# A decoder layer in which the selective scan puts four states of 32 channels on the partitions, and GpSimd's product waits for one thing fewer

## The reference

```python
# 1. linear attention, 16 heads of 32, in chunks of 128 tokens
q, k, v = x @ Wq, x @ Wk, x @ Wv               # then rotary on q and k
out = (q*decay) @ kv + ((q @ k.T) * dmask) @ v # kv carried from chunk to chunk
x1  = norm(x + rms_norm(out) @ Wo)
# 2. a selective scan over ctx [4, 512, 256]: 512 channels, 16 states each
u   = silu(causal_conv(ctx @ in_w.T) + conv_b)
dt_low, Bm, Cm = split(u @ xp_w.T)             # 16 + 16 + 16 rows per token
dt  = softplus(dt_low @ dt_w + dt_b)
for t in range(512):
    state = state * exp(dt[t]*A) + (dt[t]*u[t])[:, None] * Bm[t]  # [512, 16]
    y[t]  = sum over the 16 states of state * Cm[t]
x2  = norm(x1 + (y + D*u) * silu(x1))
# 3. 64 experts of width 192, top 8, capacity 256 rows each
w, e = top_8(softmax(x2 @ router.T));  slots from the counts so far
out  = norm(x2 + sum of w * expert_e(x2))
```

## Time and profile before

| | us |
|---|---|
| runs shown (3) | 1634.18 median, 1626.55 to 1635.15 |
| profiled execution | 1628.64 |
| its span, first to last instruction | 1626.8 |
| DVE busy | 1154.4 (71%) |
| PE busy | 1257.4 (77%) |
| POOL busy | 971.2 (60%) |
| ACT busy | 846.7 (52%) |
| mean granted TensorE clock | 0.886 |

### The profile page before, as it was taken

The page is one execution under the profiler, slowest core; times in us unless marked ns, Lnnn a source line. Parts: engine busy times, 40 slices in busy tenths (PEclk is TensorE's granted clock), DMA queues, the critical chain, the costliest instruction groups (busy, mean ns, idle before and its releaser), DMA issues. The chain is left out here.

```text
span 1626.8 us, 19387 instructions
## 1 busy us (share of the span) xinstructions
PE 1257.4 (77%) x6567; PEld 850.5 (52%) x6567; DVE 1154.4 (71%) x1554; ACT 846.7 (52%) x1417; POOL 971.2 (60%) x740
## 2 busy tenths in 40 slices
PE   1697998877898787888777661099999999999960
PEld 1243544444444353344443341099988888888850
DVE  0277988769787768877786743088878878878855
ACT  1455555642365534366423320078777777777742
POOL 0148646563886645885738824447776766767741
PEclk9978998978998898998888865589999999999985
DMA  9155545363585353664543420389999999999978
GB/s 336 66 195 183 209 146 215 134 220 110 131 205 197 110 207 123 154 197 170 192 142 108 162 82 1 102 243 304 303 294 296 292 294 292 291 294 294 292 142 309
DMA packets 146705, 326.92 MB, mean 201 GB/s; under 512 B 19504, under 2 KB 55232, under 8 KB 146480
## 3 DMA queue, kind: packets, MB, share of 16 engines
q1 hardware_dynamic: 113280, 258.41, 49.6%
q0 software_dynamic: 32768, 67.26, 17.3%
q10 hardware_dynamic: 560, 0.02, 0.0%
HBM read 273.20 MB, written 52.43 MB: 200 GB/s over the span
## 5 line engine op out<-in xcount | busy, mean ns | idle before, releaser
L849 POOL TENSOR_TENSOR dbu<-bmat,dtu 128x1024 f32<-128x1024 f32 x128 | 301.9, 2363 | 178.8 <-PE y_ps L315 62.6
L990 DVE TENSOR_TENSOR_SCAN hst<-hst,dbu 128x512 f32<-128x512 f32 x256 | 299.3, 1215 | 140.5 <-POOL dbu L849 109.0
L315 PE MATMUL y_ps<-dbu,cs 128*128 128x512 f32 x512 | 288.5, 693 | 102.3 <-DVE y L1006 63.8
L1484 POOL DMA_INDIRECT sum_rows<-ye,tokens x128 | 205.5, 1606 | 117.3 <-ACT ye L1554 88.1
L315 PEld LDWEIGHTS y_ps<-dbu,cs 128*128 128x128 f32 x512 | 101.9, 213 | 223.4 <-issue 103.0
L628 ACT ACTIVATE hst<-dt,a_sc 128x512 f32<-128x512 f32 x256 | 165.8, 683 | 90.6 <-DVE dbu L998 90.1
L364 PE MATMUL ring<-wqkv,xT 128*128 128x512 f32 x384 | 189.2, 639 | 23.7 <-DVE x L1065 13.2
L1476 POOL DMA_INDIRECT xe<-x_rows,tokens x128 | 159.4, 1246 | 56.3 <-issue 37.7
L926 POOL DMA_INDIRECT slot_table<-pairs,idx_s x128 | 125.6, 981 | 111.4 <-DVE idx_s L1159 73.4
L1618 DVE TENSOR_TENSOR w1l<-w,w1h 128x1024 fp32r<-128x1024 f32 (+1 forms) x128 | 117.2, 957 | 76.7 <-ACT w1h L1567 53.6
L998 DVE TENSOR_TENSOR dbu<-hst,cmat 128x1024 f32<-128x1024 f32 x128 | 156.7, 1224 | 11.0 <-DMA cmat<-bc_rows 6.7
(11 more groups left out here) (207 smaller groups left out, 2627.4 us busy)
## 6 DMA issues: line engine op xcount, KB each, us to landing
bmat<-bc_rows SPq DMA_DIRECT2D x128, 512.0 KB
cmat<-bc_rows SPq DMA_DIRECT2D x128, 512.0 KB
w<-in_L_ffn_gate_up_proj SPq DMA_DIRECT2D x64, 768.0 KB
w<-in_L_ffn_down_proj SPq DMA_DIRECT2D x64, 256.0 KB
w<-in_L_ffn_down_proj SPq DMA_DIRECT2D x128, 128.0 KB
rows<-sum_rows SPq DMA_DIRECT2D x8, 1024.0 KB, 12.9
sum_rows<-junk SPq DMA_DIRECT2D x1, 4608.0 KB, 23.8
x_in<-in_x SPq DMA_DIRECT2D x16, 256.0 KB, 4.1
```

Source lines behind the costliest of these rows:

```text
L315: ins = pe.matmul(y_ps[:, :], ident, dbu[:, n % WORK, i, :], start=(k == 0 and i == 0), stop=(k == UNIT - 1 and i == 1))
L849: pool.tensor_tensor(dbu[:, n % WORK, :, :], bmat[:, n % BSETS, :, :], dtu[:, m, :].unsqueeze(1).broadcast_to([P, 2, T]), ALU.mult).then_i ...
L990: dve.tensor_tensor_scan(h, h, dbu[:, n % WORK, i, :], 0.0, ALU.mult, ALU.add).then_inc(scanned, 1)
L1484: pool.indirect_dma_start(sum_dram[e % SUMS], bass.IndirectOffsetOnAxis(ap=tokens[:, e, j:j + 1], axis=0), ye[:, e % YE, j, :], None, comp ...
```

## The change

**Layout of the scan.** A slot now holds one quad of states (k = 0 to 3) of two groups of 32 channels: partition = 4 states x 32 channels, and the free dimension is 2 groups x 512 tokens. A unit is two halves (64 channels each) of four slots, so it has 8 slots as before, with two scans of 128x512 in each. `bmat` and `cmat` have a place for each quad and are loaded once per sequence: 4 transfers of 32 partitions for each of B and C and quad. In exchange `dt` and `dt*u` must stand four times below one another: SP copies them from SBUF to SBUF, 8 transfers of 64 KB each for `dt_rep` and 8 for `dtu_rep` per half (`spread_steps`, `spread_inputs`), double buffered, issued up to a half ahead. PE sums the four states by a product with `sel` (128x32, ones where p mod 32 matches), one per 32 channels, into 32 rows of `y_ps`. All four waits of `inputs` but the one for `scanned` have a counterpart.

**Set-up.** The block `setup` is gone. The host hands over weights already laid out (`layout`), x and ctx also transposed, so that PE does not turn them; the zeros go out in unit 1 (`clear_sums`); ACT scales `wo` (`weigh_rows`) after the first decays.

**Order.** `EARLY` is m = 0, 1 and `LATE` m = 2, 3. The next sequence's context projection and convolution sit in slots 0 to 5 of c = 2, `project_u` at its end; `second_sum` and `soft_rest` move one place back. `scatter` sends one store per slot from slot 2 of c = 2 on, through c = 3 and the next sequence's c = 0 and c = 1 (two or three per slot in the last sequence's c = 2 and c = 3).

```diff
-UNIT = PAIRS
+UNIT = 2 * QUADS
-EACH = 3
-EARLY, LATE = (0,), (1, 2, 3)
+EARLY, LATE = (0, 1), (2, 3)
@@ PE, sum_states
-                for i in range(2):
-                    pe.wait_ge(yc_ready, products(2 * n + i + HSTATES))
-                    ins = pe.matmul(y_ps[:, :], ident, dbu[:, n % WORK, i, :], start=(k == 0 and i == 0),
-                                    stop=(k == UNIT - 1 and i == 1))
+                pe.wait_ge(yc_ready, products(2 * n + 2))
+                for g in range(2):
+                    rows = slice((2 * half + g) * QP, (2 * half + g + 1) * QP)
+                    ins = pe.matmul(y_ps[rows, :], sel, dbu[:, n % WORK, g, :], start=(k == 0), stop=(k == QUADS - 1))
@@ SP
-                sp.dma_start(bmat[:, n % BSETS, :, :], bc_dram[b, 2 * k:2 * k + 2, :].partition_broadcast(P))\
+                for s in range(4):
+                    sp.dma_start(bmat[s * QP:(s + 1) * QP, k, :], bc_dram[b, 4 * k + s, :].partition_broadcast(QP))\
+            def spread_steps(b, m, half):
+                i = spread_of(b, m, half)
+                sp.wait_ge(dt_ready, softened(b, m))
+                wait(sp, da_ready, 2 * QUADS * (i - 1))
+                for g in range(2):
+                    for s in range(4):
+                        sp.dma_start(dt_rep[s * QP:(s + 1) * QP, i % 2, g, :],
+                                     dt[(2 * half + g) * QP:(2 * half + g + 1) * QP, m, :]).then_inc(dt_spread[i % 2], 16)
@@ POOL, inputs
                 if k == 0:
-                    pool.wait_ge(dtu_ready, softened(b, m))
+                    spread(pool, dtu_spread, i)
-                pool.wait_ge(b_loaded[n % BSETS], 16 * (n // BSETS + 1))
+                pool.wait_ge(b_loaded[k], 64 * (b + 1))
                 wait(pool, summed, n - WORK + 1)
-                wait(pool, scanned, 2 * (n - 2) + 1)
-                pool.tensor_tensor(dbu[:, n % WORK, :, :], bmat[:, n % BSETS, :, :],
-                                   dtu[:, m, :].unsqueeze(1).broadcast_to([P, 2, T]), ALU.mult).then_inc(dbu_ready, 1)
+                pool.tensor_tensor(dbu[:, n % WORK, :, :], dtu_rep[:, i % 2, :, :],
+                                   bmat[:, k, :].unsqueeze(1).broadcast_to([P, 2, T]), ALU.mult).then_inc(dbu_ready, 1)
@@ POOL, scatter
-                        if b and c >= 2:
-                            at = UNIT * (c - 2) + k
-                            scatter(b - 1, EACH * at, EACH * (at + 1))
+                        if b and c >= 2 and UNIT * c + k >= 2 * UNIT + 2:
+                            each = 1 if not last else 2 if c == 2 or k >= 4 else 3
+                            scatter(b - 1, sent, sent + each)
+                            sent += each
+                        if b >= 2 and c < 2:
+                            each = 2 if c == 1 and k >= 6 else 1
+                            scatter(b - 2, sent, sent + each)
+                            sent += each
@@ ACT, take_mixed and take_rows
-                if t == 0:
-                    act.wait_ge(zeros_stored, 16 * (1 + SUMS))
+                if b == 0 and j == 0:
+                    act.wait_ge(zeros_stored, 16 * (1 + SUMS))
+                    act.wait_ge(table_cleared, 16)
```

632 lines of the change are left out of this document (332 added, 300 removed).

## The result

The changed kernel takes 1586.53 us (median of 4 runs, 1583.99 to 1592.61), the kernel before beside it 1630.62. The ratio is 0.973, 95% interval 0.969 to 0.978: 44 us faster. The forecast was 1523, a gain of 108 against that median. The time is inside the range, at its upper end (1588); less than half of the gain came.

What follows compares the result with a forecast made beforehand. DVE was taken to bound the loop, with its waits on top. Span 1626.8 less 26 (start) and 85 (loop 868 to 783) gives 1516, plus 7 for the median: 1523 us, range 1465 to 1588.

Steps and rivals of the forecast that it cites:

- the table: Predicted unit times in the loop: c = 0 at 44.5 to 46, c = 1 58 to 60, c = 2 52, c = 3 44.5.
- Start, -26: Before the loop: ctx loaded earlier, so POOL's first product comes at 54.4 instead of 80.4 us, gain 26.
- The copies of a half ... cost nothing there: In the loop: dt and dt*u copies are issued four slots ahead, so that lead hides them at no cost.
- the handover at 8.3 against 9 us: Where c = 3 passes to the next batch: copies take 8.3 us, hidden by two DVE slots of about 9.
- POOL or the handover: Rival, chance 0.15: POOL's load and the handover keep c = 0 and c = 3 as they were; 1559 us.
- (g): POOL's dropped wait for `scanned`: PE's sum still holds the product, so counted at 0, between -14 and +15 us.
- POOL's free product blocks DVE: Rival, chance 0.04: POOL's product, out of step with the scans, meets the q and k turns; 14 us more, 1537.
- PE's sum, -115: PE's sum over states: two column parts run at once, so PE loses about 115 us, bounds 0 and 115.
- no overlap: Rival, chance 0.06: PE's column parts do not overlap at N = 512; a third of 115 on the path, 1561 us.
- (a) to (e): Reordering in units: turned-y wait 9.2 to 1.5, slot 8's wait 7.54 to 1, c = 2's 8 us of waits gone.
- (f): Routing step in c = 1: PE's and DVE's waits (5.88 and 7.35 us) stay; only C's late rows go.
- 665 to 685: Sign to check the forecast: DVE's busy time in the loop, in us, within a loop of 760 to 810.

Runs made afterwards that it cites:

- x1: The changed kernel with the loads of lane and wo issued before the first rows are stored: 1568.86 us.
- x3: The changed kernel with the dropped wait put back (POOL's product waits for the scan two slots back): 1568.33 us.
- x12: x5 with B's and C's rows loaded for batch 0 only, not again at the handovers (later batches lack their own rows): 1523.35 us.
- x5: The changed kernel with lane and wo loaded earlier, the dropped wait back, and all quad 2 and 3 rows ahead of the copies: 1552.68 us.
- x7: The kernel before without POOL's wait for the scan two slots back, nothing else: 1633.60 us, ratio 1.0034.
- x8: The changed kernel with POOL's table stores as before, three per slot in c = 2 and c = 3: 1603.72 us.
- x11: x5 with each matmul of PE's sum issued twice, so y comes out doubled: 1571.94 us.
- x4: The kernel before with PE's sum taking only the even state of each pair: 1605.52 us, ratio 0.984.
- x6: x5 with ACT making slot 5's exponentials before copying q out, in c = 1 of batches 1 to 3: 1552.51 us.
- x9: x5 with each quad of B's or C's rows loaded by one 256 KB transfer instead of four of 64 KB: 1551.84 us.
- x10: x9 with x's tiles issued ahead of the copies and C's quads 2 and 3 issued by ACT: 1554.52 us.

## Why the prediction was wrong, point by point

The forecast missed by 63.5 us. The runs name three losses: the last loads 17.7 (x1), the dropped wait 18.2 (x3), the rows at the handovers 29.3 (x12 against x5), 65 when added up. x12, which has none of the three, is 63.2 below the changed kernel, at 1523.35.

That this is the forecast's very number is luck in part. The forecast was a span of 1516 and 7 for the median above it, and here the median is 2.3 above the profiled span (0.7 in x12). The span was missed by 68: the first scan came 19.6 late (76.3 for 56.7), the loop took 43.7 more (826.7 for 783), and 5 came behind it. Of the loop's part the c = 0 units have 34.5 (171.0 for 136.5) and the c = 1 units 20.8 (198.8 for 178); the rest came out 7 under the table, and the 5 added for the clock were not needed. In x12, too, the first scan is 4.5 late (61.2), the c = 1 units take 12.7 more than the table (190.7) and the stages behind the loop 5.5 more, and what was put too high elsewhere makes up for it.

1. *Start, -26.* Right in its steps: rows of xdbl at 30.4 for 29.4, first product at 58.7 for 54.4; the 4.3 us between are mostly the copies, 0.63 us to issue for the 0.41 taken from the loads of rows. Wrong where it ended: I followed the chain to POOL's product and took the scan for its next link, without reading what stands ahead of the scan on DVE. `lane` was in the same queue as `wo`, one entry later, and I priced only `wo` (8).

2. *"The copies of a half ... cost nothing there", and the handover at 8.3 against 9 us.* This is the step that failed by most: it priced the copies alone, and the rows' reload at nothing. I compared the copies with DVE's lead and forgot that the rows of quads 2 and 3 stand in the same queue, behind them. The runs show 29.3 us for the reload (x12), and that turning the order round does not win it back: with all rows ahead of the copies (x5) c = 0 stays at 54.3 to 54.5. The rival "POOL or the handover", which had 0.15, has the right place and a wrong cause: it named POOL's load, and it kept c = 0 and c = 3 as they were. The loss is in c = 0, behind the batch's end; c = 3 is 1.4 us over the table.

3. *(g) The dropped wait, counted at 0, bounds -14 to +15.* It is +18, outside both. The rival "POOL's free product blocks DVE" (0.04, +14) named the mechanism, an instruction of DVE held while one of POOL runs, and nearly the size, but its instructions were the turns of q and k, which x3 shows unchanged (its L1035 is 488 ns now with and without the wait, while the two instructions ahead of it went from 1124 to 1515). The stretched ones are those of the routing step. I gave it 0.04 although showed L1035 at three times its twin; what kept the product beside the scans was the very wait that the change removes. That the two were one thing I did not see. The argument for 0, that `summed` holds the product anyway, is what x7 shows of the kernel before, with 5 us for 18; the change made the sum half as long in the same step.

4. *c = 1 at 60.* Measured 65 to 67. x3 alone gives 61.1 to 63.7, x8 alone 60.6: the rest is most likely the stores, moved beside the routing step (about 2.5).

5. *PE's sum, -115.* Close as busy time (-118.6), with luck: half of 2.25 us a slot is 144 over 128 slots, and the 0.9 in the sum comes from no row. PE's lower clock most likely took the difference back. The forecast gave it no line of its own; "no overlap" priced a third of it, 38. Its worth is 19 to 25 us (x11, x4). Before, c = 2 of the later batches did not depend on it at all (x4); with the stores gone it does by 2 to 3.5 us (52.5 twice in x11, 49.0 and 50.5 in x5). With less work PE was granted a lower clock (so too in x4, and the other way in x11): the loop's mean fell from 0.89 to 0.80, and the four instructions of a slot take 1.05 us at 2.4 GHz but 1.92 at 1.2 GHz. The clock fell, as I said; whether that costs the 5 us that I added, or anything, no run here shows.

6. *Order, (a) to (e).* Right: the wait for turned y fell from 9.2 to 1.1, the wait of 7.5 at slot 8 is 0.2 to 1.9, all of it for ACT, c = 2 fell to 50.4 because of the stores (x8), c = 3 to 45.9. (The waits of "about 190" that the prediction began with come to the right sum with some luck: the 21.1 of the first scan lie before the loop, and 14.8 for ACT's copies of q and k are missing.)

7. *(f) The routing step stays.* Right; x6 shows why it can't be had by ACT's order alone: k comes 5.6 us behind q from PE, and no earlier than in x5.

Of what was to show it: DVE busy "665 to 685" was the test that failed and pointed to the cause of item 3, at 695; "waits for copies over 30 us" would not have caught it, since what was late was the rows. The first scan at 76.3, for 54 to 60, failed too.

What stays open is what sets the pace at the handover while the rows are reloaded. SP's issuing is the nearest candidate: in x5 it issues for 24 us without a pause, with the DMA engines' mean share at 0.35 to 0.72 in windows of 5 us. No run tests it alone, for x9 and x10 changed the way the rows move as well. The best version run that keeps all the work is x9, with x5 and x6 equal to it within the error: 1552, 35 us below the changed kernel and 77 below the one before.

## What to carry to other kernels

When a chain is followed to an engine, read what stands ahead of the next link in that engine's own program and in the queue that feeds it; here a cast of 0.23 us, waiting for the last load in the queue, held the first scan from 59.3 (x1) to 76.3. A wait that looks redundant because another one ends as late may be what keeps two engines from meeting: before taking it out, list what the partner would then run beside. And a saving on an engine with waits of its own counts for little: 111 us less on PE were 25 in the total.

## What the runs showed of the hardware that was not expected

- DVE's instructions on tiny tiles (4 and 32 elements a partition, one SBUF input) were held until POOL's tensor instruction ended: 1.17 and 1.00 us instead of 0.17. POOL's instructions were held in the same way: 3.31 us instead of 1.27.
- A copy of 64 KB from 32 partitions to 32 others costs SP 0.62 to 0.63 us to issue (16 in 9.9), a broadcast load of 64 KB from memory 0.43 to 0.50.
- One load of 256 KB from four rows, each broadcast to 32 partitions, keeps four or five packets in flight, at 0.25 of the 16 engines' time and 94 GB/s, and the entry behind two of them stayed 8.10 us in the queue (x10). Four loads of 64 KB, one row each, kept about 10 in flight, at 0.61 and 140 GB/s (x5).
